# First layer of a two-layer kernel: engine orders from a build-time plan, its streams split, its PSUM banks pooled

## The reference, cut to what matters

```python
xn = _layernorm(x)
x = x + _L0_attn_ref(xn, ...) + _L0_ffn_ref(xn, ...)   # RWKV6 recurrence; 16 experts, top 2, per head of 16 features
xn = _layernorm(x)
x = x + _L1_attn_ref(xn, ...) + _L1_ffn_ref(xn, ...)   # causal attention, 16 heads; 8 experts, top 2, two loops
```

## Time and profile before

| | us |
|---|---|
| median of three runs | 1489.81 (1489.26 to 1500.49) |
| the profiled execution | 1478.4 |
| its span, first to last instruction | 1477.1 |
| PE busy in the span | 1316.4 (89%) |
| DVE, ACT, POOL busy | 1146.6 (78%), 873.0 (59%), 491.5 (33%) |
| mean granted TensorE clock | 0.949 |

### The profile page before, as it was taken

How to read it: one execution, slowest core, us unless ns; L and a number is a source line. 1 busy time by engine, 2 the same in 40 slices (tenths; PEclk the granted TensorE clock), 3 DMA queues, 4 the chain that set the end, 5 groups by cost and what they waited for, 6 DMA issues and landing times.

```text
span 1477.1 us, 27810 instructions
## 1 busy us (share of the span) xinstructions
PE 1316.4 (89%) x10444; PEld 591.8 (40%) x10444; DVE 1146.6 (78%) x2765; ACT 873.0 (59%) x1169; POOL 491.5 (33%) x449
## 2 busy tenths in 40 slices
PE   5487899799879888878999999999999999999996
PEld 2122323232323223235644444544445555554432
DVE  4659678956986797588998889787888778987744
ACT  2377787778676766653356566455655556555573
POOL 5532243334423531473005352025340054500034
PEclk8689999999999999889999999999999999999999
DMA  7412322322222222257535443244442245532212
GB/s 242 128 55 81 106 89 85 101 90 85 70 86 90 96 70 69 79 172 190 141 91 147 139 124 90 77 117 115 129 122 84 74 131 151 150 106 77 73 44 55
DMA packets 137125, 155.96 MB, mean 106 GB/s; under 512 B 15744, under 2 KB 99456, under 8 KB 136608
## 3 DMA queue, kind: packets, MB, share of 16 engines
q1 hardware_dynamic: 116848, 131.16, 30.4%
q0 software_dynamic: 8192, 16.79, 3.9%
q10 hardware_dynamic: 11952, 6.23, 1.4%
HBM read 109.57 MB, written 44.56 MB: 104 GB/s over the span
## 4 chain that ended last, share of the span: by engine, by line
PE 49%; DVE 11%; ACT 3%; issue 3%; POOL 3%; DMA 2%; POOLq 0%; DVEq 0%; SPq 0%; ACTq 0%
PE ax_sums L2448 8%; PE wide L2485 4%; PE wide L2357 4%; PE sh_bank L2774 4%; PE sh_bank L2744 4%; PE wide L2759 3%; DVE wide L2386 3%; PE sh_bank L2759 2%; DVE am_top L2391 2%; PE wide L2744 2%; PE m_sums L501 2%; PE m_up L480 2%; PE wide L2774 2%; POOL slot_tokens L2641 1%; ACT ax_prob L2509 1%
## 5 line engine op out<-in xcount | busy, mean ns | idle before, releaser
L2509 ACT ACTIVATE ax_prob<-wide 128x1024 f32<-128x1024 f32 (+1 forms) x320 | 295.0, 940 | 201.4 <-PE wide L2462 116.2
L534 ACT ACTIVATE m_act_h<-m_up,const 128x1024 f32<-128x1024 f32 x256 | 276.0, 1115 | 113.5 <-PE m_up L480 101.6
L2386 DVE CUSTOM_DVE_ANT_0 wide<-wide,const 128x384 f32<-128x384 f32 (+3 forms) x512 | 237.7, 516 | 50.4 <-PE wide L2357 49.3
L2641 POOL DMA_INDIRECT slot_tokens<-xn,mr_slots x128 | 125.9, 984 | 340.3 <-PE wide L2774 99.4
L2671 POOL DMA_INDIRECT m_back<-slot_results,mr_slots x128 | 122.5, 957 | 245.0 <-DMA slot_results<-m_y 127.0
L2448 PE MATMUL ax_sums<-ax_prob,al_vs 128*32 128x512 f32 (+3 forms) x1536 | 164.5, 504 | 9.0 <-ACT ax_prob L2509 8.3
L2391 DVE TENSOR_REDUCE am_top<-wide 128x2 f32<-128x1024 f32 x128 | 155.3, 1219 | 22.2 <-PE wide L2357 21.4
L480 PE MATMUL m_up<-m_terms,w1s 96*128 96x512 bf16 x512 | 155.7, 401 | 13.0 <-ACT m_act_h L534 12.9
L592 POOL TENSOR_TENSOR m_both<-m_prod,m_both 128x512 f32<-128x512 f32 x64 | 84.1, 1317 | 217.5 <-DVE m_both L550 215.2
L501 PE MATMUL m_sums<-m_act_h,const 128*32 128x512 f32 x1024 | 147.7, 641 | 4.9 <-DVE m_both L550 2.7
L2357 PE MATMUL wide<-al_ks,al_qs 48*128 48x512 bf16 (+3 forms) x768 | 118.1, 332 | 8.9 <-DMA al_ks<-kstack 2.6
(11 more groups left out here) (370 smaller groups left out, 2379.7 us busy)
## 6 DMA issues: line engine op xcount, KB each, us to landing
m_wt<-in_experts SPq DMA_DIRECT2D x92, 384.0 KB, 3.4
m_share<-shares SPq DMA_DIRECT2D x128, 256.0 KB
m_rows<-slot_tokens SPq DMA_DIRECT2D x92, 128.0 KB
slot_results<-m_y SPq DMA_DIRECT2D x92, 128.0 KB
stack<-mp_part SPq DMA_DIRECT2D x48, 128.0 KB
m_terms<-stack SPq DMA_DIRECT2D x64, 96.0 KB, 3.7
qstack<-ap_qpart SPq DMA_DIRECT2D x48, 128.0 KB
al_qs<-qstack SPq DMA_DIRECT2D x32, 192.0 KB, 3.6
```

Of the source, the lines that this page charges most:

```text
L534: A.activation(self.act_h[:, slot, :, :], self.up[u][:, :, :], ACT.Gelu, bias=self.w("b1", 4 * half + ep, 4 * half + ep + 1)).then_inc(sel ...
L2386: p = V.tensor_tensor_reduce(tile[:, x, first:first + n], tile[:, x, first:first + n], self.w("later_s", TILE - n, TILE), -1.0, 3e38, ALU. ...
L2509: A.activation(dst, src, ACT.Exp, scale=SCALE).then_inc(*banks.empties("sum", i, u))
```

## The change

All engines take the first layer's order from a second plan, `first_layer()`, computed while the kernel is built by the same `Plan`. The tables of places go; in their place stand durations and needs of each step, and a dozen constants for the wishes. The streams are split: PE has 15 in place of 5, DVE 14 in place of 6, ACT 11 in place of 5, SP 4 in place of 3. All eight banks are one `Banks` stock of four pairs: a step that fills one bank may take any of the eight (`KEPT = 0`), `up` only the pairs at banks 0 and 2 (`HOMES`). `Plan` learns of activation tables: a step of another table is held back by `SWITCH` in its wish and counted 1.3 us longer. `mus` and the two halves of a level are one step that fills two banks. `down` waits for each of the four gelus (`banks.done("up", n, ep)`), since these now lie in two bank counters. The arithmetic, its tiles, the buffers in SBUF and the number of computing instructions and DMAs stay as they are, and so does the second layer. Core of the diff:

```diff
-SUM_USES = sorted(SUM_PLACE, key=lambda use: SUM_PLACE[use])
...
-    def tensor_sums(self):
-        for use in SUM_USES:
-            yield SUM_PLACE[use]
-            if use[0] == "down":
-                self.tensor_down(*use[1:])
-            elif use[0] == "fold":
-                self.tensor_fold(use[1])
-            elif use[0] == "out":
-                self.tensor_out(use[1])
-            else:
-                self.entry.tensor(*use)
...
+    def tensor_down(self):
+        E, e, banks = self.k.nc.tensor, self.k.pe, self.banks
+        for n, (t, hp, half) in enumerate(UNITS):
+            for j in range(2):
+                yield FIRST["down", n, j]
+                e.wait_ge(*banks.free("down", n, j))
+                for ep in range(4):
+                    e.wait_ge(*banks.done("up", n, ep))
+                for ep in range(4):
+                    p = E.matmul(banks.bank("down", n, j)[32 * ep:32 * ep + 32, :], self.w("w2", 32 * (4 * half + ep), 32 * (4 * half + ep) + 32),
+                                 self.act_h[:, (4 * n + ep) % self.ACT_SLOTS, j, :], start=True, stop=True)
+                p.then_inc(banks.filled, 1)
...
+    def __init__(self, k, c, name, plan, at, wide):
+        self.pairs = [k.ps(f"{name}_pair{n}", (P, 2, TILE), ctx=c) for n in range(plan.paired)]
+        self.singles = [k.ps(f"{name}_bank{n}", ctx=c) for n in range(len(plan.tenants) - 2 * plan.paired)]
+        self.place, self.tenants, self.wide = plan.place, plan.tenants, wide
         self.number = {use: sum(plan.place[one] == n for one in uses[:m]) for n, uses in enumerate(plan.tenants) for m, use in enumerate(uses) if plan.place[use] == n}
-        self.fills = {use: n for n, use in enumerate(sorted(plan.place, key=lambda use: AT[plan.last_fill[use]]))}
-        self.filled_at = sorted(AT[plan.last_fill[use]] for use in plan.place)
-        self.filled, self.taken = k.sem("banks_filled"), [k.sem(f"bank_taken{n}") for n in range(2 * PAIRED + 1)]
...
+    def __init__(self, banks, paired, kept=0, slack=0.02, homes=()):
+        self.steps, self.streams, self.paired, self.kept, self.slack, self.homes = {}, {}, paired, kept, slack, dict(homes)
+        self.last_fill, self.place, self.tenants = {}, {}, [[] for _ in range(banks)]
...
+                found = [(max(since, free[n], free[n + 1]), n) for n in self.homes.get(uses[0][0], range(0, last, 2)) if free[n] is not None and free[n + 1] is not None]
+                return (min(found)[0], [min(found)[1]]) if found else None
             waits = lambda n: free[n] is not None and free[n] <= since
-            found = [(max(since, free[n]), n < 2 * PAIRED and waits(n ^ 1), -n) for n in range(2 * PAIRED + 1) if free[n] is not None]
-            found = min(found, default=None)
...
+            start, _, key, stream = min((c for c in best[engine] if c[0] <= first + self.slack), key=lambda c: c[1])
+            _, takes, lag, _, fills, uses, frees, _, table = self.steps[key]
+            if switches(key, engine):
+                takes += 1.3
+            if table is not None and loaded.get(engine, "-") not in table:
...
+WINDOW = {0: 2, 2: 2, 1: 3, 3: 3}
+UNIT, FIRST_UNIT = 6.9, 22.54
+PREPARE_LEAD, DOWN_AFTER, FOLD_AFTER = 13.98, 12.99, 13.68
+TURN, FIRST_TURN = 121.25, -0.78
+WITHIN = {'low': -20.9, 'mus': -1.9, 'mixture': 3.4, 'project': 5.1, 'levels': 87.9, 'carry': 81.2, 'gn': -22.2}
+ENTRY_WISH = -71.95
+SWITCH = 5.29
+KEPT = 0
+HOMES = {'up': (0, 2)}
+SLACK = 0.03
+ENTRY_UNITS = 11.22
...
+def first_layer():
+    p = Plan(8, 4, KEPT, SLACK, HOMES)
+    pe, act, dve, pool, sp = (functools.partial(p.step, engine) for engine in ("PE", "ACT", "DVE", "POOL", "SP"))
+    plan_prepare(pe, act, dve, pool, sp)
+    plan_units(pe, act, dve, pool, sp)
+    for it in range(TURNS):
+        plan_mixtures(it, pe, act, dve, pool)
+        plan_levels(it, pe, act, dve)
+        plan_carry(it, pe, act, dve)
+        plan_gated(it + 1, pe, act, dve)
+    plan_entry(pe, act, dve, pool)
+    return p.run(), p
...
+    pool("zero", ("zero",), 10.0, 0.6, since=9.0, lag=3.2)
...
+        act("h", ("mid", i), at, 0.65, ("rest", i))
+        pool("h", ("lo", i), at, 1.1, ("mid", i))
+        sp("send", ("send", i), at, 4.0, ("lo", i), lag=2.4)
...
+def plan_units(pe, act, dve, pool, sp):
+    for n, (t, hp, half) in enumerate(UNITS):
+        i, at = n // 8, unit_at(n)
+        for j in range(2):
+            q = 2 * n + j
+            if half == 0:
+                term = 8 * i + 2 * hp + j
+                sp("terms", ("terms", term), at - 10.0, 0.47, ("send", i), *([("up", 2 * ((term - Moe0.TERM_SLOTS) // 2) + 1, 3)] if term >= Moe0.TERM_SLOTS else []), lag=3.4)
+        for ep in range(4):
+            u = 4 * n + ep
+            pe("up", ("up", n, ep), at, 0.5, *[("terms", 8 * i + 2 * hp + j) for j in range(2)], *([("gelu", *divmod(u - 3, 4))] if u >= 3 else []), lag=0.2, fills=2)
+            act("gelu", ("gelu", n, ep), at, 1.03, ("up", n, ep), *([("down", (u - Moe0.ACT_SLOTS) // 4, 1)] if u >= Moe0.ACT_SLOTS else []), lag=0.18, frees=("up", n, ep), table="g")
+        pair = n // 2
+        for j in range(2):
+            q = 2 * n + j
+            sp("shares", ("shares", n, j), at, 0.63, ("share", i), *([("product", *divmod(q - Moe0.SHARE_SLOTS, 2))] if q >= Moe0.SHARE_SLOTS else []), lag=2.3)
+            before = [("pair", pair - 1, j)] if half == 0 and pair else [("fold", pair // 2 - 1)] if half and pair > 1 else []
+            pe("down", ("down", n, j), at + DOWN_AFTER, 1.02, ("gelu", n, 3), ("shares", n, j), *before, lag=0.2, fills=1)
+            dve("product", ("product", n, j), at + DOWN_AFTER, 0.66, ("down", n, j), ("shares", n, j), *before, frees=("down", n, j))
+            if half:
+                pool("pair", ("pair", pair, j), at + DOWN_AFTER, 1.3, ("product", n, j))
+        if n % 4 == 3:
+            fold = n // 4
+            pe("fold", ("fold", fold), at + FOLD_AFTER, 1.02, ("pair", pair, 1), lag=0.2, fills=1)
+            before = [("comb", fold - 1)] if fold % 2 else [("out", i - 1)] if i else []
+            dve("comb", ("comb", fold), at + FOLD_AFTER, 0.6, ("fold", fold), *before, frees=("fold", fold))
+            if fold % 2:
+                pe("fold", ("out", i), at + FOLD_AFTER, 0.92, ("comb", fold), lag=0.3, fills=1)
...
+        pe("mus", ("mus", it, i), at, 1.14, ("lowc", it, 0, 1), ("lowc", it, 1, 1), *last, *freed, lag=0.25, fills=1, uses=[("mus", it, i, s) for s in range(2)])
...
+        if h < 64:
+            pe("levels", ("lev", it, h), at, 1.8 if h < 32 else 1.1, ready, ("zero",), *(ago("outs", NC - 1, 1) if h == 32 else []), lag=0.3, fills=1, uses=[("lev", it, h, s) for s in range(2)])
+        for s in range(2):
+            if h <= 16:
+                dve("place", ("place", it, h, s), at, 0.42, ("lev", it, h), ("selves" if h == 1 else "place", it, *([] if h == 1 else [h // 2]), s), lag=0.2, frees=("lev", it, h, s))
+            elif h == 32:
...
+        pool("scale", ("scale", c), at, 3.8, ("invert0", x // 2))
...
+    for n in range(SCATTERS_EARLY):
+        pool("scatter", ("scatter", n), at, 1.28, ("slot", PLACING - 1), ("scale", MADE[GC - 1]))
...
-            merge(prep.tensor(), moe0.tensor_up(), moe0.tensor_sums(), rw.tensor(), rw.tensor_out(), ordered=True)
+            merge(prep.tensor(), prep.tensor_turned(), moe0.tensor_up(), moe0.tensor_down(), moe0.tensor_fold(), rw.tensor_low(), rw.tensor_mus(), rw.tensor_hidden(), rw.tensor_project(), rw.tensor_values(),
+                  rw.tensor_levels(), rw.tensor_carry(), rw.tensor_out(), entry.tensor_turn(), entry.tensor_logits(), ordered=True)
```

More of the change, by code:

```diff
@@ L575, in gn_added @@
[L575 to L583 removed]
+                    v.wait_ge(*banks.full("fold", pair // 2 - 1))
+                V.scalar_tensor_tensor(self.product(pair, half, j)[:, :], banks.bank("down", n, j), self.w("b2", half, half + 1),
+                                       self.share[:, q % slots, :], ALU.add, ALU.mult).then_inc(*banks.empties("down", n, j))
@@ L643 @@
[L643 to L656 removed]
+TURNS = NT // 2
@@ new lines, in tensor_mus @@
+    def tensor_mus(self):
+        E, e, banks = self.k.nc.tensor, self.k.pe, self.banks
+        for it in range(TURNS):
+            for i in MIX_ORDER:
+                yield FIRST["mus", it, i]
+                for s in range(2):
+                    e.wait_ge(*banks.free("mus", it, i, s))
+                    e.wait_ge(*banks.done("low", it, s, 1))
+                for s in range(2):
+                    first = 32 * ((i % 4) ^ s)
+                    rows = slice(first, first + 32)
+                    E.matmul(banks.bank("mus", it, i, s), self.w(f"wx2{i}")[rows, :], self.low[s][i // 4][rows, :], start=True, stop=True).then_inc(banks.filled, 1)
```

1386 lines of the change are left out of this document (745 added, 641 removed).

## The result

| | before | after |
|---|---|---|
| median of four runs each | 1489.65 us | 1453.47 us (1449.73 to 1456.77) |
| ratio of the two, 95% interval | | 0.974 [0.969, 0.979], faster |
| the profiled execution | 1478.4 | 1456.77 |
| first layer, first matmul to second meeting | 596.8 | 553.0 |
| second layer, to the end of the span | 849.0 | 871.2 |

The last line compares unlike executions: whatever the kernel, the untouched second layer took 849 to 852 us in some profiles (where the runs of the kernel before have a median of 1474 to 1476) and 865 to 871 in others (median 1490 to 1492), and the profile of before is of the first sort, that of the changed kernel of the second. So I repeated both side by side.

What follows compares the result with a forecast made beforehand. First layer's steady part bound by PE plus about an eighth idle from order and bank ownership. 1478.4 - 43 - 6 - 8 + 2 = 1423 profiled, 1435 us median; range 1407 to 1474, forecast proper 1412 to 1452 (0.58).

Steps and rivals of the forecast that it cites:

- rival (1): Level stretches: another in-order engine, DVE, becomes the bound; gain half as large, 1455 to 1472; 0.22 together with the table-cost rival.
- The steady part, -43: First layer's steady part: pooled banks and split streams cut PE's idle share from 12.5% to 5%, gaining 43 us.
- The clock, -6: Steady part: granted clock rises from 0.94 to 0.97, shortening PE's busy time by 6 us, bounds 0 and 14.
- The start, -8: Start: recurrence work moves into PE's 14.7 us hole before the first up, gaining 8 us.
- The tail, 0: End of the last turn: the plan moves group norm and scatters without shortening them; 0 us, bounds -5 and +5.
- Added waits, +2: PE: at most 192 more waits, since each down asks for four gelus in two counters; costs 2 us.
- Tables "about as many": ACT: the number of activation table loads should not rise, as the plan counts 1.3 us for each.
- The carrier's waits under 5 us: Profile after: the levels' one-column carrier matmul on PE (L731 before) waits under 5 us in total.
- No idle time over 5 us behind the logits: Profile after, start: PE has no idle time over 5 us behind the logits, where a 14.7 us hole was.
- PE's waits for the recurrence only change their releaser: Sign of a wrong prediction: PE still waits for the recurrence, with only the engine that ends the waits changed.
- (6): Banks 0 to 3: a slow tenant blocks an up pair, ups fall to a ring of one; 0.08 with the no-change rival.
- (5): Turns' meeting points, 80 in all: fixed order makes PE wait 1.5 us each for late inputs; 1505 to 1520; chance 0.06.

Runs made afterwards that it cites:

- owned banks: Changed kernel, same streams and wishes, but the banks have three owners again instead of one common stock: 1481.16 us, ratio 1.003 to the kernel before.
- short POOL: Changed kernel with seven POOL operations of the first layer cut to 64 of 512 columns, results only partly computed: 1398.58 us, ratio 0.949 to the kernel before.
- factor out: Changed kernel with eleven wish constants from the retuned kernel, but DVE durations in the plan without the factor 1.13: 1488.49 us, ratio 0.997 to the kernel before.
- retuned: Changed kernel with the plan's DVE durations times 1.13 and eleven wish constants chosen anew for the shortest plan: 1419.18 us, ratio 0.962 to the kernel before.
- banks kept: Changed kernel with the four banks of the up pairs holding only ups (KEPT = 4): 1456.96 us, ratio 0.988 to the kernel before.
- factor alone: Changed kernel with only the plan's DVE durations times 1.13, same wishes: 1455.33 us, ratio 0.985 to the kernel before.

## Why the prediction was right or wrong

Sign, place and size class were right: 1453.5 lies in the range and the gain is in the first layer alone. It is 42 to 44 us there, not the 55 of the sum, and 1453.5 stands just outside the forecast's own 1412 to 1452, on the side of rival (1). That last is within the scatter: the ratios of the two repeats, 0.972 and 0.971, applied to the 1489.65 of before would give about 1447.

That the sum came so near is in part luck. The idle time of the steady part was overrated by 23 us; the clock gave 3 more than its term, the start 4, and the 2 us of added waits did not show. These leave the 13 us between 55 and 41.8.

- **The steady part, -43: the step that failed.** It took 5% idle "nearest to the second layer's row because its mechanism is the same". Measured were 8.9% and 9.2%, and the idle time fell by 20.3 us. What went is the waits behind ACT (28.7 to 4.5 us, with the stock; back at 33.2 with owned banks). What stayed is the waits behind DVE, 29.6 and 30.1 us, most of them for a bank that DVE reads late. The term allowed for "what is late next" without a size, and took the size from a layer with other work. Rival (1) is right in its share, 8 to 10%, and in that DVE now ends most of PE's waits, 30.1 us of 43.8: with POOL's steps short, which makes DVE's shorter, the waits behind DVE fall to 12.7 us. Its place, the level stretches, holds for the second turn and not as a whole, since in DVE's fullest stretches PE went from 152 to 169 us of 192. "DVE would be 84% busy" was nearly met over the whole steady part (413.9 of 509.5, 81%), and an average over it says little.
- **The clock, -6:** 0.97 as forecast. The busy time fell by 9.2 us, of which some is work moved into the start.
- **The start, -8:** -12.3, by the reasoning given (turn 0's inputs first, its PE work in the hole). The first up came at 56.4 and 57.1, 3 to 4 later than forecast, and the gain was larger all the same; undone, it costs 21.2. The term was sized by the hole and left out what an earlier turn 0 does to the rest of the layer. It also hid part of the miss in the steady part.
- **The tail, 0:** right, within 1 us.
- **Added waits, +2:** no row shows them; the waits of L432 fell. Not settled beyond that.
- **Tables "about as many":** wrong. The first layer has 32 loads for 24, 10 us more of ACT, because the split streams let gelus and other functions alternate more often. No wait of PE at L432 for ACT is over 0.4 us in the changed kernel, so no row points to a cost.
- **Claims for the profile after.** First matmul to second meeting 550 to 554, at the outer end of 535 to 550 or past it. The carrier's waits under 5 us: 13.9 in the repeat, for 23.1 before, so over. No idle time over 5 us behind the logits: held, 2.6 is the largest in the start. Second layer unchanged: in the pair, 851.6 before and 850.0 after. Of the signs of being wrong, "PE's waits for the recurrence only change their releaser" came true in part: the carrier's own waits fell, but the sum of all that DVE ends did not.
- **Rivals.** (6), an up's bank in a slow tenant's hands, turned out as a gain. (5), the fixed order against scattering durations, is real in kind: three orders made by the same planner lose 21 to 39 us against their plans even with DVE's length put right, and one of them comes out at the old time (1488.5). That the changed kernel's order is one that holds up could not be read from the profile of before. Its list has 14 meeting points a turn, 56 in all, and not 80, so its 55 waits of 1.5 us would have been nearly every one.
- The 11.4 us between the profiled execution and the median were taken over as a constant. The larger part of it is the difference between a short and a long second layer (849 and some 865), and it was right to carry it.

## What to carry to other kernels

An order written by a planner gains as much as the buffers let it: here the same planner and wishes with owned banks gained nothing. A stock whose banks are handed out while the kernel is built is only as good as the planned durations, since a late reader holds up the one use that was given its bank. Size what remains from the stage's own waits, sorted by the engine that ends them, and not from another stage that uses the same planner. Give the planner durations as measured beside the other engines' work, then run several of its orders, since two orders of equal planned length differed by 10 us (by 20 in their medians) on one chip, and two whose plans, with DVE's length corrected, lay 3.7 us apart came out 28 apart (on two chips, between which the changed kernel's first layer differs by 4).

## What the runs showed of the hardware

- DVE steps of the recurrence take longer beside POOL's work, in the mean of a line up to twice as long: L1088 685 ns in the changed kernel and 349 with POOL's steps short, L1061 607 and 350, L985 636 and 446, while L491, with its main input in PSUM, keeps 741 and 744. Three steps of L1088 took 2.78 us beside two POOL operations of 1.31 and 1.21 us, and 1.11 us beside the same two cut to 0.36 and 0.41:

```profile
135.57 2.78 DVE L1088 SCALAR_TENSOR_TENSOR rw_state<-rw_state,rw_total,rw_add 128x128 f32<-128x128 f32 x3
135.72 1.31 POOL L530 TENSOR_TENSOR m_both<-m_prod,m_both 128x512 f32<-128x512 f32 x1 [0.82 <-DVE m_both L491]
136.99 1.21 POOL L244 TENSOR_TENSOR mp_h<-mp_h,mp_part 128x512 f32<-128x512 f32 x1
```

```profile
125.72 1.11 DVE L1088 SCALAR_TENSOR_TENSOR rw_state<-rw_state,rw_total,rw_add 128x128 f32<-128x128 f32 x3
125.89 0.36 POOL L530 TENSOR_TENSOR m_both<-m_prod,m_both 128x64 f32<-128x64 f32 x1 [1.29 <-DVE m_both L491]
126.21 0.41 POOL L244 TENSOR_TENSOR mp_h<-mp_h,mp_part 128x64 f32<-128x64 f32 x1
```

- PE's busy time is no constant of the code: the same 4352 matmuls of the first layer took 483.1 us at a granted clock of 0.97 (short POOL) and 518.7 at 0.90 (factor out). The clock falls with PE's idle time only roughly: 0.97 at 31 us idle (short POOL) and 49 (retuned), 0.94 at 68 (banks kept), but 0.90 at 63 (factor alone) and 0.92 at 92 (the kernel before).
- One and the same second layer took 849 to 852 us in all profiles of one chip, 865 to 866 in those of another, and 849.0 and 871.2 in the first two profiles. It has as many instructions each time, with a granted clock of 0.97 to 0.98 in the short ones and 0.96 to 0.97 in the long ones; PE is busy 795 to 799 us in the former and 801 to 810 in the latter. The cause is open.
